# One queue for each band: a depthwise 7x7 convolution whose band matrices are loaded by alternating DMA queues

## The reference

```python
w_sym = (weight + rot90(weight, 1) + rot90(weight, 2) + rot90(weight, 3)) * 0.25   # (192, 1, 7, 7)
x = x + depthwise_conv(_ln_c(x), w_sym, stride 1, pad 3)     # _ln_c: mean and variance over the 192 channels
t = _to_tokens(x)                                            # (16, 1024, 192)
t = t + ffn(_ln_t(t), W1, b1, W2, b2)
# ffn: y = einsum(x, sign(W1 - group mean)) + b1, scaled by a largest value per 3 images, exact gelu,
#      the same again with W2; 5 groups of 3 images, and the 16th image has ffn = 0
x = _from_tokens(t, x)
```

## Time and profile before

| | us |
|---|---|
| three timed runs | 697.81, 699.06, 699.81 |
| median | 699.06 |
| profiled execution, its own time | 697.41 |
| its span, first to last instruction | 695.6 |
| TensorE busy (share of the span) | 510.0 (73%) |
| VectorE busy | 455.9 (66%) |
| ScalarE busy | 383.2 (55%) |
| mean granted TensorE clock | 0.884 of full speed |

### The profile page before, as it was taken

How to read it: one execution, slowest core, us unless ns; L and a number is a source line. 1 busy time by engine, 2 the same in 40 slices (tenths; PEclk the granted TensorE clock), 3 DMA queues, 4 the chain that set the end, 5 groups by cost and what they waited for, 6 DMA issues and landing times.

```text
span 695.6 us, 9929 instructions
## 1 busy us (share of the span) xinstructions
PE 510.0 (73%) x3552; PEld 356.9 (51%) x3552; DVE 455.9 (66%) x1106; ACT 383.2 (55%) x612; POOL 217.0 (31%) x195
## 2 busy tenths in 40 slices
PE   4254179995299874656778979997999799778763
PEld 4254179995299873323334535554555455345342
DVE  8988922221068587599888686788878878644432
ACT  3799710000000301443799989997999799787400
POOL 4000100000000000000056756475656557678900
PEclk9778589998599995788999999999999999989865
DMA  8997136654254519900011000131222333142444
GB/s 221 304 333 186 53 82 172 167 167 138 87 149 130 152 49 362 340 0 0 13 55 47 24 24 0 47 91 64 74 69 91 96 109 92 47 135 73 135 138 155
DMA packets 55270, 81.29 MB, mean 117 GB/s; under 512 B 7161, under 2 KB 38905, under 8 KB 55222
## 3 DMA queue, kind: packets, MB, share of 16 engines
q1 hardware_dynamic: 40416, 68.93, 32.2%
q10 hardware_dynamic: 14806, 11.73, 5.7%
HBM read 53.12 MB, written 27.53 MB: 116 GB/s over the span
## 4 chain that ended last, share of the span: by engine, by line
PE 37%; ACT 22%; DVE 17%; DMA 10%; issue 5%; POOL 3%; ACTq 3%; SPq 2%; POOLq 0%; DVEq 0%
PE bank L873 15%; ACT arena L486 9%; ACT arena L480 6%; PE bank L947 5%; DMA arena<-kz_d 5%; DMA arena<-x 4%; DVE am L745 4%; POOL arena L373 3%; DVE arena L726 2%; PE bank L922 2%; DVE arena L672 2%; PE bank L924 2%; ACT arena L504 2%; PE bank L923 2%; ACT arena L466 2%
## 5 line engine op out<-in xcount | busy, mean ns | idle before, releaser
L373 POOL TENSOR_TENSOR arena<-arena 128x512 f16<-128x512 f32 x180 | 204.2, 1174 | 297.3 <-DVE arena L741 297.3
L873 PE MATMUL bank<-arena 128*128 128x112 f32 (+1 forms) x1152 | 137.1, 283 | 45.1 <-DMA arena<-kz_d 29.2
L873 PEld LDWEIGHTS bank<-arena 128*128 128x128 f32 x1152 | 135.5, 199 | 46.7 <-issue 27.0
L480 ACT ACTIVATE arena<-bank,b1s 128x512 f32<-128x512 f32 x180 | 126.1, 703 | 57.4 <-PE bank L924 57.0
L947 PE MATMUL bank<-arena 128*128 128x512 f16 x360 | 110.0, 402 | 30.4 <-ACT arena L504 19.0
L486 ACT ACTIVATE arena<-arena,gm 128x1024 f32<-128x1024 f32 x90 | 102.6, 1161 | 5.6 <-DVE gm L767 5.6
L656 DVE TENSOR_TENSOR arena<-bank,arena 128x512 f32<-128x512 f32 x48 | 33.2, 691 | 103.7 <-PE bank L873 103.6
L745 DVE TENSOR_REDUCE am<-arena 128x1 f32<-128x3072 f32 x30 | 100.3, 3343 | 0.0
L922 PE MATMUL bank<-arena 128*128 128x512 f16 x180 | 71.2, 396 | 33.9 <-DVE arena L734 14.5
L429 ACT ACTIVATE arena<-arena,wmean 51x576 f16<-51x576 f32 (+1 forms) x10 | 7.6, 840 | 136.1 <-DVE wmean L625 136.1
L947 PEld LDWEIGHTS bank<-arena 128*128 128x128 f16 x360 | 34.0, 101 | 79.3 <-issue 35.2
(11 more groups left out here) (115 smaller groups left out, 655.2 us busy)
## 6 DMA issues: line engine op xcount, KB each, us to landing
arena<-park_d SPq DMA_DIRECT2D x44, 384.0 KB, 3.4
arena<-kz_d SPq DMA_DIRECT2D x100, 112.0 KB, 2.8
arena<-kz_d ACTq DMA_DIRECT2D x92, 112.0 KB, 3.2
park_d<-arena SPq DMA_DIRECT2D x6, 1536.0 KB, 13.9
arena<-x SPq DMA_DIRECT2D x8, 1024.0 KB, 8.6
out<-arena SPq DMA_DIRECT2D x32, 256.0 KB, 2.0
kz_d<-arena SPq DMA_DIRECT2D x8, 672.0 KB, 11.3
arena<-x SPq DMA_DIRECT2D x16, 256.0 KB, 9.8
```

Source lines behind the costliest of these rows:

```text
L373: last = pool.tensor_tensor(out=low_half(u, m, m + 1), in0=yslot(u)[:, 2 * m:2 * m + 2, :], in1=hib(u, m, m + 1), op=ALU.subtract)
L480: act.activation(yslot(s)[:, 2 * m:2 * m + 2, :], m1p[c % 2][:, :].rearrange("p (h n) -> p h n", h=2), ACT.Identity, bias=b1s[:, m:m + 1], ...
L873: last = t.matmul(ps[:, :, lo:hi], WB[BUFS[g]][:, 1 - db, c, :], xn[:, :, lo + db:hi + db], start=(db == 0), stop=(db == -1))
```

## The change

SyncE now issues all four pieces of bands 0, 1 and of every even band. ScalarE issues all four pieces of every odd band from 3 on. Buffers, waits, matmuls and the ten weight transfers stay as they are. The number of pieces is the same, 192: 100 from SyncE and 92 from ScalarE, before and after. The lines of the changed kernel behind L298 are one higher, those behind L435 two.

```diff
@@ -295,7 +295,8 @@
             for done in st_ker:
                 sp.wait_ge(done, 32)
             for u in range(NCG):
-                load_bands(sp, u, range(RB) if u < 2 else range(RB // 2))
+                if u < 2 or u % 2 == 0:
+                    load_bands(sp, u, range(RB))
 
             sp.wait_ge(cev, NCG)
             for k in range(KEPT // 2, PAIRS):
@@ -431,7 +432,8 @@
             for done in st_ker:
                 act.wait_ge(done, 32)
             for g in range(2, NCG):
-                load_bands(act, g, range(RB // 2, RB))
+                if g % 2 == 1:
+                    load_bands(act, g, range(RB))
                 if g == 25:
                     act.wait_ge(conv, 24)
                     for q in range(GROUPS):
```

## The result

| | before | after |
|---|---|---|
| median of four runs, us | 698.61 (697.81 to 699.81) | 704.96 (703.82 to 705.76) |
| ratio after / before | | 1.0088, 95% interval 1.0066 to 1.011 |
| the same in later runs (17 and 6) | 697.73 | 704.57, ratio 1.0091 (1.0072 to 1.011) |
| profiled execution, own time and span, us | 697.41, 695.6 | 705.76, 704.0 |

The change costs about 6.3 us where 3.2 were forecast, twice as much. The median of 704.96 us lies inside the range that should hold 8 in 10 (698.3 to 706.0), but above the forecast's own range (700.5 to 704.5), and it is nearer to rival A's 706.2 than to the forecast's 702.3.

The account below looks back on a forecast made before the run. TensorE was taken as the mid-stage limit, with bands in time but not by much. Terms 1.2 + 1.3 + 0 + 0.7 gave +3.2 us, 702.3 us on the median; the 8-in-10 range was 698.3 to 706.0.

Parts of the forecast that it names:

- rival A: Mid stage: a band takes 5.2 us and outlasts its budget; +7.1 us in all, 706.2 us, chance 0.11.
- The band itself: Any band from one queue: four issues in a row make it take 4.7 us instead of 4.0, 0.7 slower.
- the sign that the queues slow each other though they are issued in turn: Both queues' pieces landing 3.4 us and more after issue would make the prediction wrong altogether; 2.6 to 2.8 was expected.
- Term 1: Start, two buffers: the waits for bands 2 and 4 grow by 0.7 and 0.5; +1.2 us, ends +0.9 and +2.3.
- Term 2: Mid stage: late bands such as 7, 12 and 17 cost more; +1.3 us, ends 0 and +3.0.
- The delay falls on pieces that are no longer crowded: Mid stage, late bands: the reason for taking +1.3 us instead of the +1.7 worked out.
- the budget: Mid stage, three buffers: a band must arrive within two groups, 5.36 us; slack shrinks from 1.1 to 0.4 us.
- Term 3: Weight transfers: group 26 runs under the stall, -2.7; band 27 lands later, +1.1; extra SyncE pieces, +1.6; sum 0 us.
- the 190: Weight stage: group 27 should start within 1 us of 190, plus the shift from the start and mid stage.
- Term 4: Signs: band 39, issued by ScalarE once the mean is there, takes longer; +0.7 us, ends +0.5 and +1.3.
- Four pieces in a row take 4.6: Band 39 at the signs: ScalarE's four pieces take at least 4.6 us, where 3.9 were taken before.

Follow-up runs that it names:

- The run of this part alone: Kernel before, with one queue per band in one range only: bands 2 to 5 (Term 1), ratio 1.0023; bands 6 to 25 (Term 2), ratio 1.0009.

## Why the prediction was right, and where its sizes were off

The direction holds, and so does the mechanism that was forecast: a band from one queue takes longer by the two further issues, the places where the path runs through a band pay it, and mid stage mostly hides it. It is half of what happened. Two further costs were not in the working: TensorE's clock falls behind the longer waits, and the two queues meet. That the time still lies in the range owes something to the range, which is 7.7 us wide. The term sizes, by the ends of the groups in the profiles of all runs (nine profiles with the old order at that place and five with the new at the start; nine and five, five and four, six and four at the others; single profiles scatter by 1 to 2 us; the start is counted from the start of group 0):

| term | forecast | measured, new minus old |
|---|---|---|
| 1, start (up to group 5) | +1.2 | +3.0 |
| 2, mid stage (groups 6 to 25) | +1.3 | +2.5 |
| 3, weights (groups 26, 27) | 0 | -0.5 |
| 4, signs (group 39) | +0.7 | +2.6 |
| sum | +3.2 | +7.6 (timed: +6.3, 5.0 to 7.7) |

**The band itself: right.** Forecast 4.7 us instead of 4.0, so 0.7 more. The medians in mid stage, counted from the end of the group that frees the buffer, are 4.2 with two and two and 4.9 with one queue. In the profile above the 80 pieces of bands 6 to 25 land after 2.7 us in the median (3.0 before), and 13 of them take 3.4 us or more, fewer than the 20 of before; so the sign that the queues slow each other though they are issued in turn did not come in mid stage. Rival A's 5.2 us per band did not come either, though its total of +7.1 is nearer to the timed +6.3 than the forecast is: the number alone would have spoken for the wrong mechanism. In mid stage it would have made every third group wait.

**Term 1: the waits right, the clock missing.** The two waits grow by 0.7 and 0.8 us on average, 1.4 against 1.2 forecast. That the second is above its 0.5 goes with band 4, which takes 5.1 to 5.3 us in these five profiles and not 4.7: ScalarE issues band 5 in the same 2 us. No run takes these two apart. I took a group behind a wait at 2.94 us. But TensorE's clock, which the profile of before shows falling behind the long stall, also falls behind these short waits: group 4 took 4.3 to 4.5 us in all five profiles with the new start and over 4 in three of nine with the old, group 2 in two of five and none of nine. The profile of before was one of the six in which neither was slow. On average groups 2 and 4 take 0.7 and 1.1 us more, which is the missing part. No run varies the wait alone, but the 28 cases in the 14 profiles stand in order: below 1.8 us of wait none of 15 groups was slow, from 1.8 to 2.1 four of seven were, above that all six. The run of this part alone measured +1.6 (0.1 to 3.0), so the time does not prove more than the forecast; the profiles do.

**Term 2: right in kind, at the upper side of its range.** "The delay falls on pieces that are no longer crowded" was the step that failed. Single pieces of 4.4 us (band 13 above) are hardly faster than before, when they were 4.3 and 5.0, and with a slack of 0.3 instead of 1.0 us, six to nine of the 20 bands outlast the budget instead of none to three. Of the 37 late bands in these five profiles 23 have an instruction fetch in their last 3 us, as band 7 had the earlier trace rows. The others are four bands, again and again: band 24 (and twice 18), one of whose issues takes 1.2 to 1.5 us instead of 0.6 while a 16 KB fetch runs, and band 25 (and twice 6), which meets the other queue's next band. That the fetch is the cause is argued from this coincidence. Part of the 2.5 costs nothing: the weights are issued when group 23 ends, so a wait at group 24 or 25 only shortens the stall behind it. Up to group 23 it is +2.0. The run of this part alone (+0.6, up to +1.9) still leaves term 2's size open by time.

**Term 3: right.** Band 27 takes band 26's place. From the first weight issue to the last landing that TensorE waits for it was 187.3 - 160.3 = 27.0 us before and 195.07 - 166.23 = 28.8 after: +1.8, where the forecast had 1.1 + 1.6. Less the 2.7 for group 26 that makes -0.9 in this pair of profiles. On average over the profiles, from the end of group 23 to the start of the first group behind the stall, it is 26.7 us before and 29.4 after, the forecast's +2.7, and the net is 0.0; how it divides between its two losses no run shows. Group 27 starts at 195.2 us, and less the 6.0 us by which the weights are issued later that is 189.2, within 1 us of the 190. One reading of the working was off: TensorE idles 19.5 us there and not 16, and starts at half clock as forecast. Time saw nothing (+0.4, -0.6 to +1.4), as forecast.

**Term 4: the wrong step.** "Four pieces in a row take 4.6" is what one queue does while the other is silent. At this place it is not: from the end of group 38 to band 39's last landing it is on average 6.0 us instead of 3.9, and 4.4 with the two queues taken apart. So 0.4 us are the issues, less than forecast, 1.6 us the collision, and the remaining 0.5 the clock. I had priced the odd bands on ScalarE there, and looked at SyncE's even bands only for whether somebody waits for them, not for when they are issued.

What the second queue saved here is 0.7 us per band, of two issues worth 1.2, out of a slack of 1.0 us. The Trainium skill ("DMA: Bandwidth & Descriptors", section "Issuing engines are not separate DMA queues") says that this saving of issue time is all that several issuing engines bring, and that it is "usually small relative to the DMA itself". The runs agree with the first, since 0.7 us is no more than the issue time; the second does not help here, since 0.7 us is most of the slack.

## What to carry to other kernels

Splitting one buffer's load over two queues shortens that buffer's latency by its issue time; giving whole buffers to queues in turn moves the same bytes and lengthens each latency, so count the latency against the buffer's budget before doing it, with the worst piece seen, not the median. What matters more is what stands between the pieces in a queue's program: a load behind slow transfers or behind a wait for another engine holds everyone, and moving those few loads to the queue that is free gave 18 us here (668.74 against 687.06), three times what the change cost. Where two queues wait for things that follow from the same step of the program, look whether they issue at the same moment; here they did at band 39 and at band 25. And a late buffer in front of a stall that starts on something else costs nothing.

## What the runs showed of the hardware

- Ten transfers of 51 and 38 partitions took 13 us to issue, single issues up to 5.4 us, and landed within 26 us of the first issue. The same bytes, cut so that the large parts have 48 and 32 partitions, took 8 us to issue and landed within 14 us, and the kernel was 12 us faster (11 by the medians).
- Waits of only 1.9 and 2.7 us on TensorE were followed by a granted clock of 0.63 and 0.65 in the next group, at a cost of 1.6 and 1.4 us on top of the wait. In other executions a wait of 2.0 us was followed by a group at full speed (2.93 us), and below 1.8 us every group was.
- Four 112 KB pieces from one queue alone land 2.6 to 2.8 us after their issue. With four from the other queue in the same 2 us, the slowest take 4.5 to 4.6.
- A 16 KB instruction fetch by DMA took 0.9 to 1.6 us here. Of the 19 late bands in the nine profiles with two and two in mid stage, 18 have a fetch in their last 3 us.
